# Decay-weighted scores in linear attention: the next round's products between the turnings of this one, on causal positions alone

## The chip, the cores and the metric

The kernel runs on one core of one Trainium2 chip. The metric is the device time of one execution in microseconds, from several runs of the same program. Beside it stands one profiled execution, from which all rows of the trace are taken; "the span" is the time from its first to its last instruction.

## What is computed

A small vision tower on 32 images: patch tokens, 37 positions of 256 channels each, then a layer with gated delta-rule attention and a feed-forward part, then a layer with softmax attention and a mixture of experts. The change touches only the first attention. Its core, for each of 16 heads of 16 channels and for each batch entry, is this recurrence:

```python
def step(Sst, inp):
    qt, kt, vt, bt, gt = inp
    Sd = gt[..., None, None] * Sst
    kS = jnp.einsum('bhk,bhkv->bhv', kt, Sd)
    Snew = Sd + jnp.einsum('bhk,bhv->bhkv', kt, bt[..., None] * (vt - kS))
    ot = jnp.einsum('bhk,bhkv->bhv', qt, Snew)
    return (Snew, ot)
```

The kernel doesn't carry the 16×16 state. It first computes, for each batch entry b and head, all products of keys with keys and of keys with queries over pairs of positions (t, s), weights them with the decay between s and t (and with beta for the keys), and then solves for the updates position by position. Only pairs with t at or after s are read later.

## The kernel before

Sizes: B = 32 batch entries, S = 37 positions, 128 partitions; the 16 heads are 4 groups of 4 (HG, HJ). Everything happens in one program, in which each engine has its own instruction list; the order is written out by hand, with semaphores between engines. `plan_tiles` numbers every PSUM tile in the order in which TensorE fills them; tile number n lies in bank n mod 8, `fill(key)` waits until the tile eight numbers earlier has been emptied, `full` waits for a filled tile, and `after` for an emptied one. So a tile's place in this list sets both TensorE's order and which evacuation it has to wait for.

The stage around the change has four rounds, j = 0 to 3, one for each head of a group:

- VectorE (`mask_keys(j)`, lines 1386 and 1387) makes copies KM and KML of the fp16 high and low parts of the keys, in which all channels but those of head j are zero: eight operations for the two channel halves c and two groups g. One event, `km`, is raised when all eight are done. Before round j + 1's copies are written, the last product of round j must be through.
- TensorE (`product`, lines 1647 to 1649) multiplies for each half c and batch entry b the keys and queries (weights, 128 partitions × 74 columns) with the masked keys (74 columns): three fp16 matmuls each, 2 × 32 × 3 = 192 for a round. They fill twelve tiles ("A", j, c, n) of 5 or 6 batch entries.
- ScalarE (line 1077) copies each of these tiles, 74 partitions × 370 or 444 elements, into the scratch ASB, which has two buffers, by parity of j. In ASB a partition is a pair (key or query, position t), and the free dimensions are s (37) and then 128 columns (4 groups × 32 batch entries). A copy reads 37 neighbours in PSUM and writes them 128 words apart.
- TensorE then turns the scratch (line 1783), after all twelve copies of the round: for each s one fp32 transposition, with the 128 neighbouring columns as weights and the 74×74 identity as moving operand. The result has (group, batch entry) on 128 partitions and 2 × 37 columns. Six positions share a tile ("AT", j, n), n = 0 to 6, the last has one.
- VectorE (line 1404) multiplies each turned tile with the decay weights that lie in AB[:, j] and writes the product back there. GpSimd has filled these weights beforehand; its last operation in this part ends at 165.8 us.

TensorE's order is: round 0's twelve A tiles, its seven AT tiles, round 1's twelve, its seven, and so on. After the last AT tile, TensorE loads the right-hand sides into PSUM (line 1790), and the recurrence starts with VectorE's copy at line 1429. The weights of the feed-forward part are loaded by DMA once the last A tile is emptied; they are needed later.

Other lines that the prediction speaks of: 1740 and 1741 turn beta and decay (fp16 weights of 32 columns, taken with a step of 37 elements, one column tile of the array for each of four groups), 1764 and 1765 do the same with the values; 1797 is one fp32 matmul of two columns with 128 weight columns (mean_ones); 1667 has 32 weight columns in fp32; 1853 multiplies fp32 weights of 128 columns with a 128×128 identity; 1112 copies PSUM to SBUF without steps.

## Time and profile before

| | us |
|---|---|
| median of 3 runs (lowest to highest) | 979.72 (977.64 to 984.0) |
| the profiled execution | 978.75 |
| its span | 977.0 |
| first product of round 0 to last turning of round 3 | 54.4 (170.6 to 225.0) |
| loading the right-hand sides | 4.1 (225.0 to 229.1) |

How to read it: PE is TensorE's matmuls and PEld its weight loads, which overlap them; DVE is VectorE, ACT ScalarE, POOL GpSimd. A matmul record lasts longer than its share of the engine, since records overlap: the pace is the distance from one start (or end) to the next. In the windows of rows 2, 9, 10 and 11 the columns are start and end, length, then busy time and records of each engine, granted clock, DMA share and GB/s; the number behind x counts the records that touch the window. PEclk is the clock that TensorE was granted, as a share of its full 2.4 GHz; its two levels are 1.0 and 0.5, and a window that holds both shows a value between.

### The profile page before, as it was taken

Reading aid. Unit: us, or ns where it says so; the run is one execution under the profiler, and the core shown is the slowest. Engines: PE = TensorE matmul, PEld = TensorE weight load, DVE = VectorE, ACT = ScalarE, POOL = GpSimd, SP = SyncE. Lnnn points to the kernel's source line nnn. Section 1 sums busy time; section 2 is a strip of 40 time slices with the busy share of each in tenths; the row PEclk is TensorE's granted clock in tenths of the full one; section 3 lists DMA queues with packets and bytes.
Section 4 is the critical chain, followed back from the end, with each engine's and each line's share of the span. In section 5 each row is a group of like instructions: output and inputs, shape, how many; then the busy total and the mean of one; then the engine's idle time right before and its main releaser. Section 6 shows DMA issues by size and latency. Waiting matters only on the chain.

```text
span 977.0 us, 19140 instructions
## 1 busy us (share of the span) xinstructions
PE 797.1 (82%) x7446; PEld 607.2 (62%) x7446; DVE 631.3 (65%) x916; ACT 424.5 (43%) x596; POOL 250.8 (26%) x224
## 2 busy tenths in 40 slices
PE   2864954887998866967597878569999998999997
PEld 1542733884544454745386767347877787888885
DVE  3693699468877576787767565656667755454544
ACT  6243652761024242566357663345555532223222
POOL 6000497001689921000302431013333300000000
PEclk9976985789999987987897555799999999999999
DMA  7000000002000000000130110014444422222221
GB/s 279 1 1 1 3 1 1 3 2 87 0 1 0 1 1 1 1 34 1 33 65 17 50 35 18 1 33 158 143 143 148 149 62 63 62 62 69 67 62 50
DMA packets 24355, 46.59 MB, mean 48 GB/s; under 512 B 2637, under 2 KB 10573, under 8 KB 23917
## 3 DMA queue, kind: packets, MB, share of 16 engines
q1 hardware_dynamic: 24301, 45.82, 15.2%
q8 instruction: 40, 0.66, 0.3%
q14 instruction: 14, 0.11, 0.0%
HBM read 42.51 MB, written 1.36 MB: 45 GB/s over the span
## 4 chain that ended last, share of the span: by engine, by line
PE 66%; DVE 18%; ACT 7%; issue 4%; POOL 4%; DMA 1%; DVEq 0%; POOLq 0%; ACTq 0%
PE psum L1647 10%; PE psum L1648 10%; PE psum L1649 10%; PE psum L1803 6%; PE psum L1813 4%; PE psum L775 4%; PE psum L776 4%; PE psum L777 4%; ACT arena L1077 3%; PE psum L1965 2%; PE psum L1929 2%; DVE arena L1342 1%; PE psum L1783 1%; PE psum L1853 1%; PE psum L1981 1%
## 5 line engine op out<-in xcount | busy, mean ns | idle before, releaser
L1647 PE MATMUL psum<-xh,arena 128*128 128x296 f16 (+1 forms) x664 | 196.0, 295 | 13.6 <-issue 4.9
L1648 PE MATMUL psum<-xl,arena 128*128 128x296 f16 (+1 forms) x664 | 195.9, 295 | 0.0
L1649 PE MATMUL psum<-xh,arena 128*128 128x296 f16 (+1 forms) x664 | 195.8, 295 | 0.0
L775 PE MATMUL psum<-arena 128*128 (+3 forms) x340 | 92.9, 273 | 6.0 <-DVE arena L643 6.0
L698 DVE TENSOR_TENSOR arena<-psum,arena 128x592 f32<-128x592 f32 x64 | 49.6, 775 | 69.8 <-PE psum L1649 61.2
L776 PE MATMUL psum<-arena 128*128 (+3 forms) x340 | 92.8, 273 | 0.0
L777 PE MATMUL psum<-arena 128*128 (+3 forms) x340 | 92.7, 273 | 0.0
L602 ACT ACTIVATE arena<-arena 128x592 f16<-128x592 f32 x68 | 47.4, 696 | 102.6 <-DVE arena L637 102.6
L643 DVE TENSOR_TENSOR arena<-arena 128x592 f16<-128x592 f32 x68 | 52.7, 775 | 59.0 <-ACT arena L602 58.9
L1647 PEld LDWEIGHTS psum<-xh,arena 128*128 (+2 forms) x664 | 66.1, 100 | 35.1 <-issue 15.2
L1647 PE MATMUL psum<-arena 128*74 128x74 f16 (+3 forms) x348 | 60.4, 235 | 33.0 <-POOL arena L897 18.2
L597 ACT ACTIVATE arena<-psum 128x592 f32<-128x592 f32 x68 | 44.7, 657 | 89.9 <-PE psum L1649 89.8
L564 POOL TENSOR_TENSOR arena<-arena 128x768 f32 x28 | 45.9, 1641 | 141.8 <-ACT arena L575 141.8
L637 DVE TENSOR_TENSOR arena<-arena 128x592 f32<-128x592 f32 x68 | 76.8, 1129 | 7.9 <-ACT arena L597 1.0
L1649 PEld LDWEIGHTS psum<-xh,arena 128*128 (+2 forms) x664 | 66.2, 100 | 20.4
L1648 PEld LDWEIGHTS psum<-xl,arena 128*128 (+2 forms) x664 | 66.2, 100 | 18.7
L1803 PE MATMUL psum<-arena 128*128 128x512 f32 (+1 forms) x160 | 65.3, 547 | 12.8 <-DVE arena L503 12.8
L922 POOL TENSOR_TENSOR arena<-arena 128x64 f32<-128x64 f32 (+23 forms) x24 | 43.6, 1815 | 84.1 <-ACT arena L1088 67.0
L1647 PEld LDWEIGHTS psum<-arena 128*74 128x74 f16 (+2 forms) x348 | 40.8, 123 | 36.6 <-issue 21.3
L1648 PE MATMUL psum<-arena 128*74 128x74 f16 (+3 forms) x348 | 60.2, 235 | 0.0
L1649 PE MATMUL psum<-arena 128*74 128x74 f16 (+3 forms) x348 | 60.0, 235 | 0.0
L503 DVE TENSOR_TENSOR arena<-arena,psum 128x320 f32<-128x320 f32 (+7 forms) x67 | 54.1, 808 | 6.7 <-PE psum L1803 6.7
(320 smaller groups left out, 1723.4 us busy)
## 6 DMA issues: line engine op xcount, KB each, us to landing
arena<-comb SPq DMA_DIRECT2D x64, 296.0 KB, 3.3
arena<-in_wmoe SPq DMA_DIRECT2D x34, 384.0 KB, 3.0
arena<-in_xt SPq DMA_DIRECT2D x4, 864.0 KB, 10.0
arena<-in_w SPq DMA_DIRECT2D x2, 1024.0 KB, 6.5
arena<-arena SPq DMA_DIRECT2D x6, 187.0 KB
arena<-in_ctrl SPq DMA_DIRECT2D x1, 1056.0 KB, 9.1
out<-arena SPq DMA_DIRECT2D x2, 512.0 KB, 3.1
arena<-in_wlin SPq DMA_DIRECT2D x1, 768.0 KB, 4.5
```

Of the source, the lines that this page charges most:

```text
L503: return eng.tensor_tensor(dst[:, 0:w * HJ * DH].rearrange("p (t j v) -> p t j v", j=HJ, v=DH), a_, u, ALU.mult)
L602: act.activation(ah[:, s_], t1, ACT.Copy).then_inc(ev["ah"], 1)
L637: dve.tensor_tensor(t1, t1, sg, ALU.mult).then_inc(ev["a"], 1)
L643: dve.tensor_tensor(al[:, s_], t1, ah[:, s_], ALU.subtract).then_inc(ev["al"], 1)
L698: dve.tensor_tensor(t1v, up, cb_[:, s_].rearrange("p (c t) -> p c t", c=2), ALU.mult).then_inc(ev["t1"], 1)
L775: pe.matmul(dst, hi, W[:, i, s_, 0, 2 * D:3 * D], start=start and t % 2 == 0, stop=False, skip_group_check=True)
L776: pe.matmul(dst, hi, W[:, i, s_, 1, 2 * D:3 * D], start=False, stop=False, skip_group_check=True)
L777: ins = pe.matmul(dst, lo, W[:, i, s_, 0, 2 * D:3 * D], start=False, stop=stop, skip_group_check=True)
L1647: pe.matmul(dst, wh, mh, start=start, stop=False)
L1648: pe.matmul(dst, wh, ml, start=False, stop=False)
L1649: return pe.matmul(dst, wl, mh, start=False, stop=stop)
L1803: pe.matmul(row(g0, g1 - g0), negident, ring[:, n_ % RING, 64 * (g0 - base):64 * (g1 - base)], start=False, stop=s_ + 1 == g0, skip_group_ ...
```

## The change

The order of the tiles is now written as one list, AORDER. Round 0's twelve product groups come first; then, in rounds 1 to 3, two product groups of round j alternate with one turned tile of round j − 1 (the last place has two); round 3's seven turned tiles end the list. The masks are made and signalled by channel half, so that `km` is raised twice for a round, and the first half of round j + 2 is made in the midst of VectorE's products of round j. The scratch ASB has positions innermost: 128 columns, then 37 positions s. The turning of position s reads its 128 weight columns with a step of 37 words, and is written as an ordinary matmul with the columns (i, t ≥ s0) of the identity, where s0 is the first position of the tile; so it yields 2 × (S − s0) columns, and tiles have 6 × 74, 62, 50, 38, 26, 14 and 1 × 2 columns. VectorE multiplies only these and writes them to their places.

```diff
--- before.py
+++ after.py
@@ -126,12 +126,8 @@
             add(("n2r", m, q), "dve")
     for n in range(5):
         add(("vT", n), "dve")
-    for j in range(HJ):
-        for c in range(2):
-            for n in range(len(ASPLIT)):
-                add(("A", j, c, n), "act")
-        for n in range(7):
-            add(("AT", j, n), "dve")
+    for key in AORDER:
+        add(key, "act" if key[0] == "A" else "dve")
 
     for g in range(len(GROUPS)):
         place[("R", g)] = (len(place), "row", GROUPS[g][1])
...
 ASPLIT = [6, 6, 5, 5, 5, 5]
 ASTART = [sum(ASPLIT[:i]) for i in range(len(ASPLIT))]
+AT_AFTER = {(0, 1): (0,), (0, 3): (1,), (0, 5): (2,), (1, 1): (3,), (1, 3): (4,), (1, 5): (5, 6)}
+AORDER = [key for j in range(HJ + 1) for c in range(2) for n in range(len(ASPLIT)) for key in
+          ([("A", j, c, n)] if j < HJ else []) + [("AT", j - 1, x) for x in (AT_AFTER.get((c, n), ()) if j else ())]]
+
+
+def at_group(n):
+    s0 = 6 * n
+    return s0, min(6, S - s0), 2 * (S - s0)
 
 
 def tower(nc, a, out, probe=None):
@@ -369,7 +373,7 @@
 
         AB = carve(19100, HJ, 2, S, S)
         bvt = carve(12032, S, HJ, DH)
-        ASB = carve(0, 2, S, 128, parts=74)
+        ASB = carve(0, 2, 128, S, parts=74)
         KM = carve(30052, 2, B, 2, S, dt=F16)
         KML = carve(9472, 2, B, 2, S, dt=F16)
         ring = carve(0, RING, 64 * (S - 8))
@@ -1072,8 +1076,8 @@
                     for n in range(len(ASPLIT)):
                         full(act, ("A", j, c, n))
                         b0, nb = ASTART[n], ASPLIT[n]
-                        src = bank(("A", j, c, n))[0:74, 0:nb * 74].rearrange("p (b g s) -> p g b s", b=nb, g=2)
-                        dst = ASB[:, j % 2].rearrange("p s (g b) -> p g b s", g=HG)[:, 2 * c:2 * c + 2, b0:b0 + nb, :]
+                        src = bank(("A", j, c, n))[0:74, 0:nb * 74].rearrange("p (b g s) -> p b g s", b=nb, g=2)
+                        dst = ASB[:, j % 2].rearrange("p (g b) s -> p b g s", g=HG)[:, b0:b0 + nb, 2 * c:2 * c + 2, :]
                         act.activation(dst, src, ACT.Copy).then_inc(emptied["act"], 1)
 
             def weight_sums():
@@ -1376,35 +1380,36 @@
                     "p (t j v) -> p t j v", j=HJ, v=DH), beta, ALU.mult).then_inc(emptied["dve"], 1)
                 after(dve, ("vT", n_))
 
-            def mask_keys(j):
+            def mask_keys(j, c):
 
                 if j:
-                    full(dve, ("A", j - 1, 1, len(ASPLIT) - 1))
-                for c in range(2):
-                    for g_ in range(2):
-                        one = hm[:, 4 * g_ + j:4 * g_ + j + 1]
-                        link(dve.tensor_scalar(KM[:, c, :, g_, :], kqh[:, c, :, 0, :], one, None, ALU.mult), hold=False)
-                        ins = dve.tensor_scalar(KML[:, c, :, g_, :], kql[:, c, :, 0, :], one, None, ALU.mult)
-                        if c and g_:
-                            ins.then_inc(ev["km"], 1)
-                            dve.wait_ge(ev["km"], j + 1)
-                        else:
-                            link(ins, hold=False)
+                    full(dve, ("A", j - 1, c, len(ASPLIT) - 1))
+                for g_ in range(2):
+                    one = hm[:, 4 * g_ + j:4 * g_ + j + 1]
+                    link(dve.tensor_scalar(KM[:, c, :, g_, :], kqh[:, c, :, 0, :], one, None, ALU.mult), hold=False)
+                    ins = dve.tensor_scalar(KML[:, c, :, g_, :], kql[:, c, :, 0, :], one, None, ALU.mult)
+                    if g_:
+                        ins.then_inc(ev["km"], 1)
+                    else:
+                        link(ins, hold=False)
 
             dve.wait_ge(ev["vl"], 2)
-            mask_keys(0)
+            mask_keys(0, 0)
+            mask_keys(0, 1)
+            mask_keys(1, 0)
             for j in range(HJ):
                 if j + 1 < HJ:
-                    mask_keys(j + 1)
+                    mask_keys(j + 1, 1)
                 for n_ in range(7):
-                    s0, ns = 6 * n_, min(6, S - 6 * n_)
+                    if n_ == 3 and j + 2 < HJ:
+                        mask_keys(j + 2, 0)
+                    s0, ns, w = at_group(n_)
                     full(dve, ("AT", j, n_))
                     dve.wait_ge(ev["decay"], j + 1)
-                    dst = AB[:, j, :, :, s0:s0 + ns].rearrange("p i t s -> p s i t")
-                    dve.tensor_tensor(dst, bank(("AT", j, n_))[:, 0:ns * 74].rearrange(
-                        "p (s i t) -> p s i t", i=2, t=S), dst, ALU.mult).then_inc(emptied["dve"], 1)
-                    if n_ == 6:
-                        after(dve, ("AT", j, n_))
+                    dst = AB[:, j, :, s0:S, s0:s0 + ns]
+                    dve.tensor_tensor(dst, bank(("AT", j, n_))[:, 0:ns * w].rearrange(
+                        "p (s i t) -> p i t s", i=2, t=S - s0), dst, ALU.mult).then_inc(emptied["dve"], 1)
+            after(dve, ("AT", HJ - 1, 6))
 
 
             def reduce_o(t):
@@ -1764,25 +1769,26 @@
                         pe.matmul(dst, seq(vh[:, hg // 2])[:, :, t], pick, start=True, stop=False)
                         ins = pe.matmul(dst, seq(vl[:, hg // 2])[:, :, t], pick, start=False, stop=True)
                 ins.then_inc(filled[who(("vT", n_))], 1)
-            for j in range(HJ):
-                pe.wait_ge(ev["km"], j + 1)
-                for c in range(2):
-                    for n_, nb in enumerate(ASPLIT):
-                        ps = fill(("A", j, c, n_))
-                        for i in range(nb):
-                            b = ASTART[n_] + i
-                            ins = product(ps[0:74, 74 * i:74 * i + 74], kqh[:, c, b].rearrange("p i s -> p (i s)"),
-                                          kql[:, c, b].rearrange("p i s -> p (i s)"),
-                                          KM[:, c, b].rearrange("p i s -> p (i s)"),
-                                          KML[:, c, b].rearrange("p i s -> p (i s)"), True, True)
-                        ins.then_inc(filled[who(("A", j, c, n_))], 1)
-                after(pe, ("A", j, 1, len(ASPLIT) - 1))
-                for n_ in range(7):
-                    ps = fill(("AT", j, n_))
-                    for s_ in range(6 * n_, min(6 * n_ + 6, S)):
-                        ins = pe.transpose(ps[:, 74 * (s_ % 6):74 * (s_ % 6) + 74], ASB[:, j % 2, s_, :],
-                                           ident[0:74, 0:74])
-                    ins.then_inc(filled[who(("AT", j, n_))], 1)
+            for key in AORDER:
+                ps = fill(key)
+                if key[0] == "A":
+                    _, j, c, n_ = key
+                    pe.wait_ge(ev["km"], 2 * j + c + 1)
+                    for i in range(ASPLIT[n_]):
+                        b = ASTART[n_] + i
+                        ins = product(ps[0:74, 74 * i:74 * i + 74], kqh[:, c, b].rearrange("p i s -> p (i s)"),
+                                      kql[:, c, b].rearrange("p i s -> p (i s)"),
+                                      KM[:, c, b].rearrange("p i s -> p (i s)"),
+                                      KML[:, c, b].rearrange("p i s -> p (i s)"), True, True)
+                else:
+                    _, j, n_ = key
+                    after(pe, ("A", j, 1, len(ASPLIT) - 1))
+                    s0, ns, w = at_group(n_)
+                    for x in range(ns):
+                        ins = pe.matmul(ps[:, w * x:w * x + w], ASB[:, j % 2, :, s0 + x],
+                                        ident[0:74, 0:74].rearrange("p (i t) -> p i t", i=2)[:, :, s0:S], start=True,
+                                        stop=True)
+                ins.then_inc(filled[who(key)], 1)
 
             after(pe, ("vT", 4))
             for g, (g0, g1) in enumerate(GROUPS):
```

## Rows read from the trace of the kernel before

**Rows 1.** The page: busy time of each engine; the chain that ended last, by engine.
```profile
...
PE 797.1 (82%) x7446; PEld 607.2 (62%) x7446; DVE 631.3 (65%) x916; ACT 424.5 (43%) x596; POOL 250.8 (26%) x224
...
PE 66%; DVE 18%; ACT 7%; issue 4%; POOL 4%; DMA 1%; DVEq 0%; POOLq 0%; ACTq 0%
...
```

**Rows 2.** Windows of the stage: length, each engine's busy time and records, clock, DMA.
```profile
...
core 0: us, PE busy (x) PEld busy (x) DVE busy (x) ACT busy (x) POOL busy (x), PEclk, DMA share, GB/s
...
170.60:179.40 8.80, 8.79 (x192) 8.71 (x192) 0.00 (x0) 7.10 (x10) 0.00 (x0) 0.77 0.02 4
179.40:181.20 1.80, 0.03 (x2) 0.01 (x1) 1.66 (x4) 1.74 (x3) 0.00 (x0) 1.00 0.00 0
181.20:185.60 4.40, 4.40 (x38) 4.40 (x39) 4.37 (x8) 0.00 (x0) 0.00 (x0) 0.53 0.00 0
...
195.80:198.20 2.40, 2.40 (x37) 2.40 (x38) 2.37 (x6) 0.00 (x0) 0.00 (x0) 1.00 0.00 0
...
208.10:212.40 4.30, 4.29 (x42) 4.30 (x43) 4.27 (x8) 0.00 (x0) 0.00 (x0) 0.58 0.02 4
...
220.80:222.40 1.60, 0.00 (x0) 0.00 (x0) 0.00 (x0) 1.56 (x3) 0.00 (x0) 1.00 0.00 0
222.40:225.00 2.60, 2.59 (x38) 2.59 (x39) 1.89 (x3) 0.00 (x0) 0.00 (x0) 1.00 0.67 173
225.00:229.10 4.10, 4.03 (x11) 1.61 (x9) 3.52 (x5) 0.00 (x0) 0.00 (x0) 1.00 0.97 402
...
```

**Rows 3.** VectorE's timeline before the first product: start, duration, line; and TensorE's first.
```profile
...
166.89 0.54 DVE L1386 TENSOR_SCALAR arena<-arena,hm 128x1184 f16<-128x1184 f16 x1
...
168.68 0.54 DVE L1386 TENSOR_SCALAR arena<-arena,hm 128x1184 f16<-128x1184 f16 x1
...
170.60 0.28 PE L1647 MATMUL psum<-arena 128*74 128x74 f16 x1 [11.23 <-DVE arena L1387]
...
```

**Rows 4.** Line 1647 in two stretches: count, durations, first and last start.
```profile
...
L1647 PE MATMUL psum<-arena x20: 257/258/259, 170.8 to 174.4; 128*74 128x74 f16 x20
...
L1647 PE MATMUL psum<-arena x40: 197/198/201, 174.9 to 179.1; 128*74 128x74 f16 x40
...
```

**Rows 5.** Groups by line and shape, 165 to 233 us: busy time, mean ns.
```profile
...
L1077 ACT ACTIVATE arena<-psum 74x370 f32<-74x370 f32 x32 | 22.3, 839 | 0.1
L1404 DVE TENSOR_TENSOR arena<-psum,arena 128x444 f32<-128x444 f32 x24 | 20.7, 938 | 7.6 <-issue 7.5
L1077 ACT ACTIVATE arena<-psum 74x444 f32<-74x444 f32 x16 | 14.4, 964 | 28.3 <-PE psum L1649 28.1
...
```

**Rows 6.** Line 1112: copies with contiguous output, durations.
```profile
...
L1112 ACT ACTIVATE arena<-psum x2: 437/517/597, 347.9 to 349.8; 128x512 f32<-128x512 f32 x1, 128x320 f32<-128x320 f32 x1
...
```

**Rows 7.** Line 1783: all its records.
```profile
...
L1783 PE MATMUL psum<-ident,arena x148: 227/228/333, 181.2 to 224.8; 74*128 74x74 f32 x148
...
```

**Rows 8.** Line 1797: its two records, and their piece of TensorE's timeline.
```profile
...
L1797 PE MATMUL psum<-arena,mean_ones x2: 168/210/251, 292.2 to 292.2; 128*128 128x2 f32 x2
...
292.21 0.28 PE L1797 MATMUL psum<-arena,mean_ones 128*128 128x2 f32 x2
...
```

**Rows 9.** Windows with line 1853 alone, at either clock.
```profile
...
388.88:392.20 3.32, 3.32 (x15) 3.32 (x16) 0.50 0.00 0
449.20:450.90 1.70, 1.70 (x16) 1.58 (x14) 1.00 0.00 0
...
```

**Rows 10.** Windows within lines 1740/1741 and 1764/1765; loads of lines 1740 and 1667.
```profile
...
104.40:107.30 2.90, 2.90 (x194) 2.90 (x193) 2.87 (x3) 2.79 (x3) 0.00 (x0) 1.00 0.02 6
153.10:155.00 1.90, 1.83 (x118) 1.87 (x121) 1.87 (x4) 0.83 (x1) 1.90 (x1) 0.50 0.00 0
...
L1740 PEld LDWEIGHTS psum<-identh,arena x97: 128/151/156, 104.4 to 107.2; 32*32 32x32 f16 x97
...
L1667 PEld LDWEIGHTS psum<-arena,mean_ones x32: 106/108/109, 41.3 to 618.2; 128*32 128x32 f32 x32
...
```

**Rows 11.** The attention stage as one window.
```profile
...
523.00:611.58 88.58, 69.63 (x1345) 58.76 (x1343) 52.90 (x105) 53.94 (x65) 30.08 (x22) 0.52 0.10 29
...
```

## Prediction

> **What bounds the kernel now.** I read the page first. TensorE is busy 82% of the span and carries 66% of the chain that ended last [rows 1], so whatever stretches TensorE's work in this stage is paid in full. Then the stage alone, in windows cut at its changes of work [rows 2]. It runs from 170.6 us, where VectorE has masked the first keys [rows 3], to 225.0 us, where the last turning ends; TensorE then loads the rows of the recurrence (line 1790, to 229.1 us). There are four rounds. Each is a train of 192 products (8.2 to 8.8 us), a hole of 1.3 to 2.0 us in which TensorE does nothing and ScalarE still copies, and a train of 37 turnings (4.4, 2.4, 4.3 and 2.6 us). The four holes, of which the first and the last stand in the rows, sum to 6.7 us. The clock is not constant: the turnings at 181.2 and those at 208.1 us ran at 0.53 and 0.58 of full clock, those at 195.8 and 222.4 at 1.00 [rows 2]. So the stage costs 54.4 us, of which 4 × 7.0 us would be products at full clock: 40 of line 1647's records in 4.2 us are 108 ns for each group of three, and a round has 64 groups [rows 4].
>
> VectorE and ScalarE have slack. ScalarE's twelve copies of a round take 4 × 0.96 and 8 × 0.84 us less their overlap, about 9 us; VectorE's eight masks are 3.6 us (0.45 us apart, [rows 3]) and its seven products on turned scores 5.3 us [rows 5].
>
> **The change, part by part.**
>
> *Masks by half.* The first products wait for four masks, not eight: the fifth starts at 168.68 us, 1.8 after the first, and before the change the product waited for the eighth, until 170.60 [rows 3]. TensorE starts near 168.8, 1.8 us earlier. The cold start of 8.8 us for round 0 is kept. Later masks lie beside other work: their only cover is TensorE's round, which is longer than VectorE's 8.9 us in each case below. Mask (j+1, second half) stands in VectorE's queue ahead of AT(j, 0), and costs 1.8 us there; TensorE is then in the next round's products with eight banks to fill, so nobody waits. If that cover were gone, it would be 1.8 us a round.
>
> *Interleaving.* The holes go: the copy of A(j, 1, 5) ends behind the first two product groups of round j+1, and in round 3 behind AT(2, 5) and AT(2, 6). That is worth up to 6.7 us.
>
> *Copies into the scratch.* ScalarE now writes 37 neighbours. The plain copies of line 1112 take 437 ns for 320 and 597 ns for 512 elements [rows 6], so 0.83 ns an element: a round falls from about 9 to 4 × 0.54 + 8 × 0.48 = 6.0 us. It is worth nothing on the path, since ScalarE only sets the holes that interleaving hides.
>
> *VectorE's products.* 1586 elements a round and partition in place of 2738. Off the path too.
>
> *The turning itself.* This is the dear part. Before, it is one transposition per position: 148 records for 4 × 37 [rows 7], 74 columns each, 2.4 us / 37 = 64 ns at full clock and 4.4 / 37 = 119 ns at half [rows 2]. After, it is an ordinary fp32 matmul. Line 1797 issues one of these and leaves two records, each with its weight load [rows 8]. So a round has 74 records in place of 37. Streaming: 64 ns / 74 = 0.87 ns a column; widths of 74, 62, 50, 38, 26, 14 six times each and 2 once are 1586 columns, twice: 2.75 us. Causality thus saves 42% of the columns and the second record takes it back: at best level with 2.4 us.
>
> But each record loads 128 fp32 columns as weights. Line 1797 streams two columns, next to nothing, and still its records end 0.11 us apart: the pair lasts 0.28 us, the first record 0.168 [rows 8]. Line 1853, whose weights are fp32 128×128, goes at 16 records in 1.70 us at full clock, some 0.11 us, and 214 ns at half [rows 9]. The load is thus the floor, and narrowing the moving side below 128 columns buys nothing: 74 × 0.111 = 8.2 us a round. This is the lower bound for real, against 2.4 to 4.4 us before.
>
> The upper bound comes from the new layout. With positions innermost, the 128 weights of a position lie 37 words (148 bytes) apart; before they were neighbours. The trace has no strided fp32 load. The nearest rows are lines 1740 and 1764, whose 32 fp16 weight columns lie 74 bytes apart. Four column tiles work at once there: 194 matmuls of 8 columns in 2.90 us are 60 ns per tile and matmul at full clock; 118 of 64 columns in 1.90 us are 64 ns at half clock [rows 10]. Neither the clock nor an eightfold width moves it, so it is the strided load: 60 / 32 = 1.9 ns a column, against 0.87 for contiguous fp32. The shortest load of line 1740 is recorded with 128 ns, that of 32 contiguous fp32 columns with 106, of which 32 × 0.87 = 28 are reading: (128 − 106 + 28) / 32 = 1.6 ns [rows 10]. For 128 columns these give 200 to 240 ns. I take 215 ns, between them, and also the pace of a contiguous fp32 load at half clock: 74 × 0.215 = 15.9 us a round.
>
> On the same point the Trainium skill is divided. "SBUF — State Buffer", section "Door 1: The DMA port swizzle", says that SBUF is read in lines of 16 bytes and that an access which crosses to a new line pays; by it every one of these columns pays. "TensorE: Matmul & The Clock Gate", section "LDWEIGHTS (loading the stationary operand)", prices a load by its column count alone; by it the layout is free and rival 1 below comes true. Lines 1740 and 1764 speak for the first page. "Perfetto Trace Analysis", section "Transposes", asks for real transpose operations and not standard matmuls; the 64 ns above against two loads agree.
>
> *The sum.* 168.8 + 8.8 (round 0) + 3 × 7.0 (products) + 4 × 15.9 (turnings) = 262.2 us where 225.0 was: +37.2. The last turning has no product beside it, but was always exposed. Loading the rows stays at 4.1 us.
>
> *The clock.* The products' pace falls from 36 to 63 ns a record at half clock (20 groups in 3.6 us [rows 4]), a round's from 7.0 to about 12. In the attention stage TensorE holds 1345 small matmuls, is busy 79% of the time, and the granted clock is 0.52 [rows 11]. The new stage puts product trains of 1.1 to 1.3 us between load-bound turnings of 2.6 us, which stream little. The price lies between nothing and 3 × 5 + 4 = 19 us; I take 6, a little over one round. The strided load itself does not follow the clock [rows 10]. Result: +43 on the profiled execution's 978.75 us (977.0 of span), 1022; the median of the runs lies 1 us above that execution, so 1023.
>
> **Rivals.**
>
> *1. The load is not slowed by the stride* (8.2 us a round). 168.8 + 8.8 + 21.0 + 32.8 = 231.4: +6.4, and with up to 7 us of lost clock +13: 985 to 992, point 988. For it: an fp32 column already takes two steps of the contiguous load, which may hide the line's latency; no row shows fp32 strided. Against it: rows 10.
>
> *2. Half clock from end to end.* Products 12.3 a round, loads 214 ns whatever the stride [rows 9]: 168.8 + 4 × 12.3 + 4 × 15.8 = 281, with the rows' load 4 us longer: +60, so 1039. For it: the attention stage. Against it: before, 192 products in a row always won the clock back.
>
> *3. Faster.* The load of a record hides behind the stream of another, so that only the streaming counts, 2.75 us a round. Then 168.8 + 8.8 + 3 × 9.75 + 2.75 = 209.6: −15.4, so 964. VectorE's 8.9 us would still fit. It decides at (225.0 − 168.8 − 8.8 − 21.0) / 296 = 89 ns a record: below that the change wins. Against it: lines 1797 and 1853 both stand at 111.
>
> **How the numbers follow.** Strided load 0.58, rival 1 0.25, rival 2 0.09, rival 3 0.08. The likeliest case alone spans 1012 (200 ns, full clock: +32.8) to 1044 (240 ns, all of the clock lost: +64). Rival 1 begins at 985. The range 984 to 1042 leaves out rival 3 and the ends of the others. One per cent, 9.8 us, is about what a measurement of this kernel can tell from no change. Half of rival 1 lies within it: same 0.14, faster 0.07, slower 0.79.
>
> **What would show it.** Starts of line 1647 at 168.8, not 170.6; no hole of over 0.5 us on TensorE between rounds; two records for each turning; their pace, 215 ns against 111 against under 89, which decides between the forecast and rivals 1 and 3; the pace at full and half clock alike; ScalarE's copies near 0.5 us; the first row operation (line 1429) at 266 to 275 us, not 229. Behind it all durations stay. I would be wrong if the turnings' pace is that of contiguous weights, or if the clock falls for good.

## The result and the profile after

| | us |
|---|---|
| the kernel before, median of 4 runs beside it | 979.50 (977.64 to 984.0) |
| the changed kernel, median of 4 runs | 1047.57 (1046.62 to 1048.25) |
| ratio, 95% interval | 1.068 (1.065 to 1.071) |
| span of the profiled execution, before and after | 977.0, 1044.9 |

The change makes the kernel 68 us slower. The direction was forecast, and that the slow loads make the loss; the size was 25 us short, and the time lies above the range (984 to 1042 us).

The page of the changed kernel: TensorE's busy time has grown from 797 to 873 us, the clock row has a long stretch at 5, and TensorE's share of the chain that ended last is 71% where it was 66% [rows 1].

```profile
...
PE 873.4 (84%) x7594; PEld 682.3 (65%) x7594; DVE 621.5 (59%) x916; ACT 413.9 (40%) x596; POOL 250.9 (24%) x224
...
PEclk9977967555579999979898855579999999999999
...
PE 71%; DVE 16%; ACT 4%; issue 4%; POOL 3%; DMA 1%; DVEq 0%; POOLq 0%; ACTq 0%
...
```

Windows of the changed kernel, same columns as [rows 2]: round 0's 192 products and the first 36 of round 1; all that follows up to the last turning, and of that the part at half clock; loading the right-hand sides and the first row operations.

```profile
...
core 0: us, PE busy (x) PEld busy (x) DVE busy (x) ACT busy (x) POOL busy (x), PEclk, DMA share, GB/s
168.50:179.20 10.70, 10.66 (x227) 10.69 (x228) 4.58 (x11) 6.42 (x13) 0.00 (x0) 0.72 0.01 3
179.20:288.10 108.90, 108.90 (x843) 108.90 (x839) 18.82 (x45) 17.73 (x36) 0.00 (x0) 0.53 0.05 20
184.80:288.40 103.60, 103.60 (x791) 103.60 (x791) 17.41 (x43) 16.07 (x32) 0.00 (x0) 0.50 0.06 21
288.10:298.80 10.70, 7.14 (x11) 2.99 (x11) 3.62 (x7) 0.31 (x1) 0.33 (x1) 0.66 0.00 0
...
```

The 45.6 us from 179.4 to 225.0 us before (three product trains, four turning trains, four holes) are now 108.9 us, without a hole and with 36 products fewer in them. In them the clock was full until 184.7 us and at half from there until 293.9 us, behind the last turning.

The turnings are now line 1788. Here are its records in the first stretch, of which the greater part is at full clock, and in the last one, at half; columns: count, shortest, median and longest ns, first and last start.

```profile
...
L1788 PEld LDWEIGHTS psum<-ident,arena x24: 334/356/358, 179.2 to 186.2; 74*128 74x128 f32 x24
L1788 PE MATMUL psum<-ident,arena x24: 414/420/466, 179.3 to 186.3; 74*128 74x74 f32 x12, 74*128 74x62 f32 x12
...
L1788 PEld LDWEIGHTS psum<-ident,arena x88: 343/356/361, 265.7 to 287.9; 74*128 74x128 f32 x88
L1788 PE MATMUL psum<-ident,arena x88: 388/450/513, 265.7 to 288.0; 74*128 74x14 f32 x24, 74*128 74x74 f32 x12, 74*128 74x62 f32 x12, 74*128 74x50 f32 x12
...
```

87 intervals in 22.2 us are 255 ns each. The first 24 stand in two tiles with 30 products of 1.1 us between: (7.0 − 1.1) / 23 = 257 ns. The first tile's twelve ran wholly at full clock, which fell in the midst of the second, and the starts lie 253 to 257 ns apart in both, but for each tile's first interval (285 and 275 ns). The median load takes 356 ns from start to end at either clock. A record of 74 columns and one of 2 take the same place.

Groups by line and shape of the changed kernel:

```profile
...
L1788 PEld LDWEIGHTS psum<-ident,arena 74*128 74x128 f32 x296 | 77.2, 355 | 0.0
...
L1081 ACT ACTIVATE arena<-psum 74x370 f32<-74x370 f32 x32 | 15.4, 482 | 48.8 <-PE psum L1654 48.5
...
L1081 ACT ACTIVATE arena<-psum 74x444 f32<-74x444 f32 x16 | 8.7, 546 | 34.9 <-PE psum L1654 34.7
...
```

296 loads for 148 transpositions [rows 7]; ScalarE's copies fell from 839 and 964 ns [rows 5] to 482 and 546, as worked out (0.48 and 0.54 us). TensorE's first product and VectorE's last product and first row operation on the timelines:

```profile
...
288.38 0.16 DVE L1410 TENSOR_TENSOR arena<-psum,arena 128x2 f32<-128x2 f32 x1 [0.25 <-PE psum L1788]
295.34 0.23 DVE L1434 COPY arena<-psum 128x64 f32<-128x64 f32 x1 [6.79 <-PE psum L1796]
...
168.54 0.25 PE L1652 MATMUL psum<-arena 128*74 128x74 f16 x1 [9.64 <-DVE arena L1390]
...
```

The first product starts at 168.54 us (170.60 before [rows 3]; in the profiled runs below whose masks are made by half it lies between 167.7 and 172.3 us, so that one start alone doesn't show the gain), and the first row operation at 295.34 us, where the kernel before had it at 229.1, the end of its last window [rows 2]. These 66 us are the loss; the rest of the span adds under 2 us, which I have not followed.

### The profile page after: what moved, and what is told of

Its sections match the earlier page's. It is cut to its first block, busy times and chain, and to the rows that moved or that the text cites. A ratio compares the mean times of both kernels' runs of the same rounds, so it can differ in the third digit from the quotient of the medians.

```text
span 1044.9 us, 19501 instructions
## 1 busy us (share of the span) xinstructions
PE 873.4 (84%) x7594; PEld 682.3 (65%) x7594; DVE 621.5 (59%) x916; ACT 413.9 (40%) x596; POOL 250.9 (24%) x224
## 4 chain that ended last, share of the span: by engine, by line
PE 71%; DVE 16%; ACT 4%; issue 4%; POOL 3%; DMA 1%; DVEq 0%; POOLq 0%; ACTq 0%
PE psum L1652 10%; PE psum L1653 10%; PE psum L1654 10%; PE psum L1788 7%; PE psum L1809 5%; PE psum L1819 4%; PE psum L779 3%; PE psum L780 3%; PE psum L781 3%; PE psum L1971 2%; PE psum L1935 2%; DVE arena L1346 1%; PE psum L1859 1%; PE psum L1987 1%; POOL arena L957 1%
## 5 line engine op out<-in xcount | busy, mean ns | idle before, releaser
L1652 PE MATMUL psum<-arena 128*74 128x74 f16 (+3 forms) x348 | 72.9, 260 | 30.7 <-POOL arena L901 18.0
L1788 PE MATMUL psum<-ident,arena 74*128 74x74 f32 (+6 forms) x296 | 78.8, 442 | 0.0
L1809 PE MATMUL psum<-arena 128*128 128x512 f32 (+1 forms) x160 | 66.7, 556 | 14.3 <-DVE arena L507 14.3
L1788 PEld LDWEIGHTS psum<-ident,arena 74*128 74x128 f32 x296 | 77.2, 355 | 0.0
L1653 PE MATMUL psum<-arena 128*74 128x74 f16 (+3 forms) x348 | 72.9, 260 | 0.0
L1652 PEld LDWEIGHTS psum<-arena 128*74 128x74 f16 (+2 forms) x348 | 50.7, 147 | 33.8 <-issue 30.8
```

Of the source, the lines that this page charges most:

```text
L1652: pe.matmul(dst, wh, mh, start=start, stop=False)
L1653: pe.matmul(dst, wh, ml, start=False, stop=False)
L1788: ins = pe.matmul(ps[:, w * x:w * x + w], ASB[:, j % 2, :, s0 + x], ident[0:74, 0:74].rearrange("p (i t) -> p i t", i=2)[:, :, s0:S], star ...
L1809: pe.matmul(row(g0, g1 - g0), negident, ring[:, n_ % RING, 64 * (g0 - base):64 * (g1 - base)], start=False, stop=s_ + 1 == g0, skip_group_ ...
```

## The experiments

"Near" below means that the 128 weight columns of a turning are neighbours in the scratch, "far" that they lie 37 words apart; "narrow" is the cut to causal columns, "wide" all 74. The changed kernel is far, ordinary, narrow and interleaved; the kernel before is near, transposed, wide and sequential.

### Near instead of far

```diff
-        ASB = carve(0, 2, 128, S, parts=74)
+        ASB = carve(0, 2, S, 128, parts=74)
...
-                        ins = pe.matmul(ps[:, w * x:w * x + w], ASB[:, j % 2, :, s0 + x],
+                        ins = pe.matmul(ps[:, w * x:w * x + w], ASB[:, j % 2, s0 + x, :],
```

(and ScalarE's output pattern as before the change)

> The changed kernel with one part undone: the scratch has its old layout, positions outside and 128 columns as neighbours, so that the weights of a turning lie side by side. The turning stays an ordinary fp32 matmul of two records on causal positions, interleaved as changed. Theory (the strided load costs 255 ns a record, a contiguous one 111 at full clock and 214 at half): the pace of the turnings falls to 111 ns where the clock is full; the stage ends at 168.5 + 10.7 + 21.0 + 296 x 0.111 = 233 us instead of 288, with half-clock stretches up to 245; time 985 to 1000 us, still slower than before, since two contiguous loads cost 8.2 us a round against 2.4 to 4.4. Rival (the ordinary fp32 matmul on 74 partitions is slow by itself, or the interleaving makes it so): pace and time stay at 255 ns and about 1047 us.

Measured: 1011.67 us, ratio 1.031 (1.027 to 1.034). Windows on the turnings at full and at half clock, and the loads of the whole run:

```profile
...
178.90:189.90 11.00, 11.00 (x184) 11.00 (x184) 3.83 (x9) 7.43 (x10) 0.00 (x0) 1.00 0.01 3
189.90:267.10 77.20, 77.20 (x654) 77.20 (x653) 14.09 (x35) 21.79 (x27) 0.00 (x0) 0.50 0.08 28
...
L1788 PEld LDWEIGHTS psum<-ident,arena x296: 187/333/333, 178.9 to 266.9; 74*128 74x128 f32 x148
...
```

The loads have a shortest time of 187 ns and a median of 333, not 356 throughout: contiguous loads follow the clock, with starts 112 ns apart in the first window and 214 in the second. The second window holds 238 of the 296 records and takes 77.2 us, all at half clock. By the medians the far layout is worth 36 us of the 68. The time is 12 us above the range that I expected (985 to 1000). The profiled execution took 1024.7 us, 13 more than the median; in it the clock fell at 189.9 us and stayed down until the last turning. The windows are that execution's, and the median one, with a mean granted clock of 0.865 where this has 0.856, had less time at half clock.

### Ordinary matmul or transposition, on far weights

```diff
-                                        ident[0:74, 0:74].rearrange("p (i t) -> p i t", i=2)[:, :, s0:S], start=True,
-                                        stop=True)
+                                        ident[0:74, 0:74], start=True,
+                                        stop=True, is_transpose=True)
```

(the tile has 6 × 74 columns again)

> The changed kernel with only the ordinary matmul undone: each turning is again one transposition with all 74 columns of the identity, whose 128 weight columns are read with the step of 37 words. VectorE multiplies all 74 columns as before. Theory (every strided column costs about 2 ns, whatever the mode): one record of 255 ns a position, 37 x 0.255 = 9.4 us a round; 168.5 + 10.7 + 21.0 + 37.7 = 238 us at full clock, up to 255 with the products at half clock; time 988 to 1010 us. Rival (only the two-record fp32 matmul pays for the step; in transposition mode the load keeps its 64 ns): stage ends at 210 us, time near 963 us.

Measured: 974.63 us, ratio 0.993 (0.990 to 0.996). The window from the first to the last turning, and the loads:

```profile
...
179.10:216.20 37.10, 37.10 (x694) 37.10 (x692) 22.36 (x44) 17.68 (x36) 0.00 (x0) 0.98 0.10 36
...
L1788 PEld LDWEIGHTS psum<-ident,arena x148: 189/213/231, 179.1 to 216.0; 74*128 74x128 f32 x148
...
```

37.1 us for 540 products (36 of round 1's had run before the first turning) and 148 turnings, at 0.98 of full clock. 540 × 36 ns = 19.4 leaves 17.7 us, or 120 ns a turning; within a tile the six starts lie 120 ns apart, too. Both of my expectations were wrong: not 255, not 64. The far load costs something in transposition mode too, but half as much, and a turning has one of them in place of two. This led to the theory that a load is a row of reads: a transposition reads each of its 128 columns once, an ordinary fp32 load twice, and a far read costs about 1 ns (255 / 256 and 120 / 128) where a near one costs 0.43 (111 / 256). No trace shows single reads; the theory can be tested by its prices alone.

### The load by itself

A kernel of its own: 36 fp16 matmuls of 512 columns to raise the clock, then 24 or 48 small matmuls on weights at one step, and so on for each step.

```python
for _ in range(24): pe.matmul(banks[1][0:128, 0:16],
    X[:, 0:4736].rearrange("p (a k) -> p a k", k=37)[:, :, 0], ident[:, 0:16], start=True, stop=True)
```

> A kernel of its own that computes nothing of the reference: after bursts of wide fp16 matmuls it runs rows of small matmuls whose only cost is the weight load, for fp32 in ordinary mode (two records each), fp32 in transposition mode and fp16, at steps of 1 to 40 elements between the weight columns. Theory (a load reads one element a step, an ordinary fp32 load reads each column twice, and a read that leaves its neighbourhood costs about 1 ns instead of 0.42 at full clock): fp32 ordinary 111 ns at step 1 and 255 at step 37, transposition 64 and 120; the pace rises at some small step and is flat beyond it, and it is in proportion to the number of columns (128 at 64 columns, 64 at 32). Rival (the step of 148 bytes is special, by a conflict of addresses): steps of 36, 37 and 40 words differ, and steps of 8 or 16 words cost nothing.

It was executed once. Each row is one of these series, 48 records; the pace is the distance from first to last start over 47. In order: fp32 ordinary, 128 weight columns, at steps of 1, 2, 3, 4, 5, 8, 16, 36, 37 and 40 words; 64 and 32 columns at step 37; fp16, 128 columns at steps 1 and 37; fp32 in transposition mode at steps 1 and 37.

```profile
...
L59 PE MATMUL psum<-ident,X x48: 179/263/376, 25.5 to 31.2; 128*128 128x16 f32 x48
...
L61 PE MATMUL psum<-ident,X x48: 179/268/374, 41.9 to 47.4; 128*128 128x16 f32 x48
...
L63 PE MATMUL psum<-ident,X x48: 179/360/375, 56.8 to 65.8; 128*128 128x16 f32 x48
...
L65 PE MATMUL psum<-ident,X x48: 194/394/394, 76.2 to 87.0; 128*128 128x16 f32 x48
...
L67 PE MATMUL psum<-ident,X x48: 183/381/381, 97.1 to 107.3; 128*128 128x16 f32 x48
...
L69 PE MATMUL psum<-ident,X x48: 199/396/398, 117.5 to 128.5; 128*128 128x16 f32 x48
...
L71 PE MATMUL psum<-ident,X x48: 179/375/378, 138.3 to 148.3; 128*128 128x16 f32 x48
...
L73 PE MATMUL psum<-ident,X x48: 196/393/393, 158.5 to 169.3; 128*128 128x16 f32 x48
...
L75 PE MATMUL psum<-ident,X x48: 214/413/413, 179.2 to 190.9; 128*128 128x16 f32 x48
...
L77 PE MATMUL psum<-ident,X x48: 279/481/481, 200.3 to 215.1; 128*128 128x16 f32 x48
...
L79 PE MATMUL psum<-ident,X x48: 277/278/301, 226.2 to 232.1; 128*64 128x16 f32 x48
...
L81 PE MATMUL psum<-ident,X x48: 217/218/237, 241.5 to 244.6; 128*32 128x16 f32 x48
...
L83 PE MATMUL psum<-identh,XH x48: 169/169/173, 254.2 to 255.4; 128*128 128x16 f16 x48
...
L93 PE MATMUL psum<-identh,XH x48: 173/203/205, 302.9 to 305.7; 128*128 128x16 f16 x48
...
L99 PE MATMUL psum<-ident,X x48: 272/273/273, 335.2 to 340.3; 128*128 128x128 f32 x48
...
L103 PE MATMUL psum<-ident,X x48: 273/283/283, 361.8 to 367.4; 128*128 128x128 f32 x48
...
```

The clock did not stay up in all of them: it fell within each of the ten ordinary fp32 series of 128 columns. So each must be read by its stretches of one clock. Here are steps 3 and 37, at full clock and then at half:

```profile
...
L63 PE MATMUL psum<-ident,X x24: 179/324/345, 56.8 to 60.7; 128*128 128x16 f32 x24
...
L63 PE MATMUL psum<-ident,X x25: 345/374/375, 60.7 to 65.8; 128*128 128x16 f32 x25
...
L75 PE MATMUL psum<-ident,X x19: 214/404/413, 179.2 to 183.6; 128*128 128x16 f32 x19
...
L75 PE MATMUL psum<-ident,X x30: 413/413/413, 183.6 to 190.9; 128*128 128x16 f32 x30
...
```

| weights, step in elements | pace of the series, ns | median distance of two starts, ns, at full clock | at half clock |
|---|---|---|---|
| fp32 ordinary, 128 columns: 1 | 121 | 112 | 214 |
| 2 | 117 | 118 | 213 |
| 3 | 191 | 173 | 213 |
| 4 | 230 | 233 | 233 |
| 5 | 217 | 220 | 220 |
| 8 | 234 | 238 | 238 |
| 16 | 213 | 217 | 217 |
| 36 | 230 | 233 | 233 |
| 37 | 249 | 253 | 253 |
| 40 | 315 | 320 | 320 |
| fp32 ordinary, step 37: 64 columns | 126 | 127 | 127 |
| 32 columns | 66 | 67 | |
| fp16, 128 columns: 1, 4, 8, 37 | 26, 32, 60, 60 | 25, 33, 60, 60 | |
| fp16, 32 columns: 1, 37 | 26, 60 | 25, 60 | |
| fp32 transposition: 1, 4, 37 | 109, 121, 119 | 109, 121, 120 | |

(A series' pace can lie below both distances, since its first interval is short. In the transposition series 128 columns are streamed, some 110 ns by the 64 ns that 74 columns took before, so that at step 1 the stream is the floor.)

Two things come out clearly. A load at step 1 or 2 goes with the clock. From step 4 on it costs the same at either clock, and more than a near one at full clock; at half clock, where the near load costs 214 ns itself, 16 words add 3 ns and 37 words 39. And in fp32 the far price is in proportion to the number of columns (253, 127, 67), and an ordinary load costs about twice the transposition's (233 against 121 at step 4, 253 against 120 at 37). So far the theory holds. It fails in two places. Beyond 4 words the ordinary load isn't flat: 217 ns at 16 words, 238 at 8, 320 at 40. The rival has a part in that, though 8 and 16 words are far from free; no rule came out for it. And the price per column isn't that of a read in general: 128 fp16 columns at step 37 take the same 60 ns as 32 of them.

The Trainium skill, "SBUF — State Buffer", section "Door 1: The DMA port swizzle", names lines of 16 bytes, four fp32 words, and wants two accesses in a line: steps of 1 and 2 words have that and are cheap, 3 has it at times and lies between, 4 never has it. The runs agree in this. "TensorE: Matmul & The Clock Gate" of the Trainium skill, section "LDWEIGHTS (loading the stationary operand)", by which only the number of columns counts, is contradicted: 128 fp32 columns cost 112 to 320 ns at full clock.

### Interleaving alone

The two edits above together: near, transposed, wide. What is left of the change is the order of tiles and the masks by half.

> The interleaving and the masks by half alone: scratch in its old layout, turnings as transpositions of all 74 columns, VectorE's products on all positions as before. Theory (the loss lies wholly in the turning's load, the interleaving is a gain): 64 ns a turning at full clock, 168.5 + 10.7 + 21.0 + 3 x 2.4 + 2.4 = 210 us, at worst 220 with half-clock stretches; ScalarE's copies, about 9 us a round, just fit a round of 9.4 us. Time 963 to 974 us, faster than before. Rival (the interleaving costs by itself, by waits for ScalarE's strided copies or by switching between matmul and transposition): 980 us or more.

Measured: 967.71 us, ratio 0.985 (0.981 to 0.989): faster than both kernels. A middle round (from the first turning on, so it holds the last products of one round and the first of the next), the last turnings, and the loads:

```profile
...
181.10:190.50 9.40, 9.34 (x227) 9.37 (x228) 6.06 (x13) 8.97 (x13) 0.00 (x0) 1.00 0.02 3
207.60:211.30 3.70, 3.07 (x51) 2.95 (x49) 2.55 (x6) 1.21 (x2) 0.00 (x0) 1.00 0.39 95
...
L1788 PEld LDWEIGHTS psum<-ident,arena x148: 137/142/147, 181.1 to 211.2; 74*128 74x128 f32 x148
...
```

A round is 9.4 us, full clock, TensorE busy for 9.34 of it, and ScalarE for 8.97: the copies just fit, as worked out. It beats the kernel before by 14 us.

### Wide records on far weights

```diff
-    return s0, min(6, S - s0), 2 * (S - s0)
+    return s0, min(6, S - s0), 2 * S
```

> The changed kernel with the causal cut undone and nothing else: each record of a turning streams all 74 columns and VectorE multiplies all of them. The loads are the same 296 with the same step. Theory A (the load is the floor of a record, and the clock falls because the turnings stream little): the pace stays at 255 ns, more streaming keeps the clock up for longer, product trains at 36 instead of 63 ns: up to 15 us from the products and 6 us behind them, time 1027 to 1045 us, so that more work is not slower. Theory B (the clock falls because of the loads, whatever streams): pace 255, clock at half from about 185 to 294 us as now, time 1047 us. Rival (the cut to causal columns does save TensorE time): 74 x 31 columns x 2 at 0.87 ns a round more, time 1055 us or more.

Measured: 1046.93 us, ratio 1.066 (1.060 to 1.072).

```profile
...
179.80:289.40 109.60, 109.60 (x841) 109.60 (x839) 22.96 (x45) 17.65 (x36) 0.00 (x0) 0.52 0.06 20
...
```

The cut to causal columns is worth nothing here: 2738 columns a round in place of 1586, each streamed twice, in the same time. It is no cost either, and the clock falls just as early (185.0 us, against 184.7). On far weights this is what theory B forecast.

### Wide records on near weights

The first edit (near) with this one.

> As the run with the old scratch layout and ordinary matmuls (1012 us, half clock from 190 to 272 us), but each record streams all 74 columns. Loads are the same, and below 128 columns the stream is hidden behind the load. Theory (the clock fell because the records stream little): the clock stays at full after the start; turnings 111 ns, products 36 ns; the stage ends at 168.5 + 10.7 + 21 + 33 = 233 us, time 985 to 990 us: more columns, 22 us faster. Rival (the loads or the alternation take the clock, whatever streams): clock and time as without the cut undone, 1010 us or so.

Measured: 993.09 us, ratio 1.011 (1.008 to 1.015). From the first to the last turning:

```profile
...
181.50:237.90 56.40, 56.30 (x835) 56.33 (x836) 22.19 (x43) 27.59 (x36) 0.00 (x0) 0.93 0.11 39
...
L1788 PEld LDWEIGHTS psum<-ident,arena x296: 187/192/333, 181.6 to 237.8; 74*128 74x128 f32 x148
...
```

56.4 us where the narrow records took 88.2 in their profiled execution. That one was 13 us above its median, so the windows overstate the gain: by the medians it is 19 us. The median load is 192 ns, that of full clock, where it was 333, and the mean granted clock of a whole execution is 0.881 to 0.885, where that of the narrow records is 0.853 to 0.865. The same loads, at full clock with starts 112 ns apart in both kernels, more columns, and faster: here the narrow records themselves cost the clock. The pace of the turnings is 114 ns within a tile, near the 111 that the forecast took for a contiguous load at full clock; the 993 us are close to rival 1's 985 to 992.

### Fillers

```diff
                     for x in range(ns):
+                        pe.matmul(ps[:, w * ns:512], identh[:], xh[:, 0, 0:512 - w * ns], start=True, stop=True)
```

in the changed kernel.

> The changed kernel plus one fp16 matmul ahead of each turned position, whose result nobody reads: it streams 68 to 510 columns into the part of the tile that the turnings leave free. It adds 148 matmuls and takes nothing away. Theory (half of the loss beyond the loads is the clock, which thin streams cost): the clock stays at or returns to full for most of the stage; each filler costs its load, about 55 ns, so 8 us in all; products save up to 15 us, the loading of the right-hand sides and the start of the recurrence about 6 us: 1035 to 1043 us, faster with more work. Rival (the clock is down for another reason): half clock as before, each filler dearer, 1055 us or more.

Measured: 1046.12 us, ratio 1.066 (1.062 to 1.070).

```profile
...
179.40:291.70 112.30, 112.30 (x991) 112.24 (x988) 18.87 (x45) 17.71 (x36) 0.00 (x0) 0.69 0.06 20
...
```

Neither expectation was met (1035 to 1043 us, or 1055 and more), and of the 55 ns set for a filler's load the series above shows 25, for 128 fp16 columns at step 1. The mean clock of the stretch rises from 0.53 to 0.69 and the 148 extra matmuls come free, no more: what the clock gives back is what they cost. It shows that more work between the turnings moves the clock on far weights as well, but it gives no faster kernel.

### Sequential order

```diff
-AORDER = [key for j in range(HJ + 1) for c in range(2) for n in range(len(ASPLIT)) for key in
-          ([("A", j, c, n)] if j < HJ else []) + [("AT", j - 1, x) for x in (AT_AFTER.get((c, n), ()) if j else ())]]
+AORDER = [key for j in range(HJ) for key in [("A", j, c, n) for c in range(2) for n in range(len(ASPLIT))] +
+          [("AT", j, n) for n in range(7)]]
```

(and `mask_keys(j + 1, 0)` directly ahead of `mask_keys(j + 1, 1)`)

> The changed kernel with the interleaving alone undone: twelve product tiles, then seven turned tiles, as before the change; layout, ordinary matmul, causal cut and masks by half stay. Theory (the interleaving is worth its holes, and costs the long product trains that win the clock back): turnings 255 ns; each train of 192 products starts at half clock and ends at full, about 9.5 us in place of 12; holes of 1 us a round: 168.5 + 10.7 + 3 x 9.5 + 75.5 + 4 = 287 us, as with interleaving; time 1040 to 1050 us. Rival (the interleaving is the loss): under 1020 us.

Measured: 1039.39 us, ratio 1.059 (1.055 to 1.062). The first turning train and the product train behind it:

```profile
...
182.30:201.20 18.90, 18.90 (x75) 18.90 (x76) 3.85 (x9) 0.00 (x0) 0.00 (x0) 0.56 0.00 1
201.20:210.50 9.30, 8.66 (x193) 8.55 (x194) 2.63 (x7) 6.01 (x12) 0.00 (x0) 0.80 0.01 2
...
```

37 turnings in 18.9 us are 255 ns for each of 74 records; the clock falls within the train (mean 0.56). The 192 products behind it take 9.3 us with the hole, at 0.80: in one train they win the clock back halfway. Interleaved, the changed kernel needs 44.1 us for the products of all four rounds (10.7 + 108.9 − 296 × 0.255); in sequence the four trains with their holes take 38.3 (10.1, 9.3, 9.4 and 9.5). So on far weights interleaving loses some 6 us of the stage and 8 of the whole time, and on near transposed weights it wins 14.

### Raising the clock ahead of round 0

The interleaved kernel above plus 30 unread fp16 matmuls of 512 columns while TensorE would wait for the masks.

```diff
+            for _ in range(30):
+                pe.matmul(fill(("A", 0, 0, 0)), identh[:], xh[:, 0, 0:512], start=True, stop=True)
             for key in AORDER:
```

> The interleaving alone (old scratch layout, transpositions; 968 us) plus 30 fp16 matmuls of 512 columns, whose result nobody reads, into the bank of the first product tile while TensorE would wait for the masks. They end before the masks do if the clock rises in time. Theory (round 0 costs 10.6 us in place of 7.0 because TensorE stood idle before it and got half clock): round 0 runs at 36 ns a product, the stage ends 3.5 us earlier, time 964 us, ratio to the kernel before 0.981. Rival (the masks end later than the matmuls by enough for the clock to fall again, or the matmuls delay the first product): 967 us or more.

Measured: 964.87 us, ratio 0.984 (0.982 to 0.987).

```profile
...
168.80:177.30 8.50, 8.33 (x228) 8.28 (x228) 4.67 (x11) 7.25 (x11) 0.00 (x0) 1.00 0.02 4
...
```

Round 0 and the first two groups of round 1 run at full clock, 228 products in 8.4 us where the kernel without the fillers took 10.6. Then TensorE waits for ScalarE's last copies; the first turning starts at 178.7 instead of 181.1 us, of which 1.0 us is that the first product started earlier in this execution. In total this isn't told apart from the run without (0.985): inconclusive.

### The layout alone, in the kernel before

```diff
-        ASB = carve(0, 2, S, 128, parts=74)
+        ASB = carve(0, 2, 128, S, parts=74)
...
-                        ins = pe.transpose(ps[:, 74 * (s_ % 6):74 * (s_ % 6) + 74], ASB[:, j % 2, s_, :],
+                        ins = pe.transpose(ps[:, 74 * (s_ % 6):74 * (s_ % 6) + 74], ASB[:, j % 2, :, s_],
```

> The kernel before with the layout of the scratch alone changed: positions innermost, ScalarE writes neighbours, the transposition's 128 weight columns lie 37 words apart; order and transpositions as before. Theory (a strided load costs 120 ns in transposition mode at either clock; copies shrink from 0.84 and 0.96 to 0.48 and 0.55 us): turnings 4.4 us in each round where 4.4, 2.4, 4.3 and 2.6 stood, +4 us, and the holes between products and turnings shrink by some 0.8 us each, -3 us: 978 to 983 us, the same as before. Rival (the copies count for more than the holes): 975 us or less.

Measured: 981.78 us, ratio 1.000 (0.998 to 1.003).

```profile
...
L1783 PEld LDWEIGHTS psum<-ident,arena x148: 190/213/231, 179.9 to 224.6; 74*128 74x128 f32 x148
...
L1077 ACT ACTIVATE arena<-psum 74x370 f32<-74x370 f32 x32 | 15.4, 481 | 4.3 <-PE psum L1649 3.2
L1077 ACT ACTIVATE arena<-psum 74x444 f32<-74x444 f32 x16 | 8.7, 543 | 32.9 <-PE psum L1649 26.4 <-DVE arena L1404 6.0
...
```

Loads have a median of 213 ns, where the near transposed ones of the interleaved run have 142, and the copies are 0.36 and 0.42 us shorter; gain and loss cancel, as expected.

## Why the prediction was wrong in size

*Starts, copies, records.* Right: the first product at 168.54 us (forecast 168.8), copies of 0.48 and 0.55 us off the path, two records a turning, no hole, the load as the floor whatever the width, and a far load that keeps its pace at both clocks. Rival 1 (the step costs nothing) and rival 3 fell. Not so the first row operation, which came at 295.3 us and not at 266 to 275, and of the two signs by which I would be wrong one came true: the clock fell at 184.7 us and was down beyond the last turning.

*The pace of a far load* is the first term mis-sized. I took 215 ns between 200 and 240 (step "the turning itself"); it is 255, above both bounds. 296 × 0.255 = 75.5 us against 63.6: +11.9 us. Two things went wrong in it. The lower bound came from the recorded duration of a single load and was pulled into a mean; the pace of lines 1740 and 1764 (60 ns for 32 columns [rows 10]) would have given 240. And the carry from fp16 at 74 bytes to fp32 at 148 bytes was not exact: the series give 66 ns for 32 fp32 columns against 60 for fp16. That the carry came as near as it did is partly luck: it took four times the price of 32 columns for 128, which holds in the series for fp32 (67 and 253 ns) and not for the fp16 from which it was taken (60 and 60).

*The clock* is the second. I took 6 us out of a range of 0 to 19. Measured: the products of all four rounds 44.1 us instead of 29.8 (+14.3; round 0's own 192 took 9.4 instead of 8.8), from the last turning to the first row operation 7.2 instead of 4.1 (+3.1): 17.4 us, +11.4. Rival 2 had the clock right and was given 0.09, since I held it for an alternative to the slow load. The slow load is enough to bring it about: with 74 columns a record, far weights have 0.52 of full clock in the turnings and near ones 0.93. (Narrow records on near weights bring it about, too.) The argument against rival 2 (192 products in a row win the clock back) was taken from trains that the change cuts into pieces of 30 and 36. The two terms were treated as independent, the load taken near its middle and the clock at a third of its range; 43 + 11.9 + 11.4 = 66, which is the delay of the first row operation.

*Split of the loss by runs:* from far to near weights 36 us (1047.6 to 1011.7). With both at half clock it would be 296 × (255 − 214) ns = 12 us; the rest I put down to the clock, which near loads follow and which is up for longer (a mean of 0.865 in the median execution, against 0.842), but no run takes it by itself. The cut to causal columns costs 19 us on near weights through the clock (1011.7 to 993.1) and nothing on far ones. The ordinary matmul in place of the transposition costs 25 us on near weights (993.1 to 967.7) and 72 on far ones (1046.9, wide, to 974.6). The interleaving gives 14 us with transpositions and takes 8 with far ordinary ones. The parts don't add: the far layout costs nothing in the kernel before (981.8), 7 us in the interleaved kernel with transpositions (967.7 to 974.6) and 54 with ordinary wide matmuls (993.1 to 1046.9). Ordinary matmuls lose on near weights already; the pair of them and far weights makes most of the loss.

*What stays open.* Why 37 words cost more than 16 and less than 40, and 8 more than 16. Whether an ordinary fp32 load really reads twice: its price says so, nothing else does. And what the clock goes by: more columns kept it up on near weights and not on far ones, and fillers lifted it for part of the stage; no run here gives the reason.

## What to carry to other kernels

Many small fp32 matmuls are bound by their weight loads, so look at the layout and the mode of the stationary operand before counting moving columns: a transposition loads it once and an ordinary fp32 matmul twice, and at full clock a step of 4 words or more made each ordinary load 1.9 to 2.9 times as dear (217 to 320 ns against 112). If a copy has to be strided, let it be the evacuation, which is hidden here, rather than the weights. And when a change puts load-bound matmuls among the others, price the clock of everything around them together with their load, not as an independent chance: here the load was 11.9 us of the error and the clock 11.4.

## What the runs showed of the hardware that I had not expected

- A far load keeps its pace at both clocks (255 ns at 1.0 and 0.5, as the forecast had it), while a near one goes from 112 to 214 ns. So at half clock the far step costs little: 3 ns at 16 words and 39 at 37.
- The fp32 load's price depends on the step beyond "near or far": 217 ns at 16 words, 253 at 37, 320 at 40.
- 128 fp16 weight columns at step 37 take 60 ns, as long as 32 such columns in the same series and in the kernel before, and a quarter of fp32's price in ordinary mode.
- Streaming 74 columns a turning in place of 43 on average made a kernel 19 us faster, by the clock: 0.881 to 0.885 over the whole execution, against 0.853 to 0.865.
